# Second and third attention of a decoder: keys in three tiles of 103, two heads to a column group

## The reference

```
# second attention (L0_xattn): 77 keys, q and k normalised per head
q = layernorm((x @ Wq) per head) * sqrt(8);  k, v = (ctx @ Wkv) per head, k layernormed
attn = softmax(q @ k.T);  out = (attn @ v) @ Wp + bp
# third attention (L1_xattn): 77 keys, no bias; masked keys are left out
scores = (x @ W_q.T) @ (ctx @ W_k.T).T / sqrt(8), -inf where mask[key]
attn = softmax(scores), 0 where a row is all masked;  out = (attn @ (ctx @ W_v.T)) @ W_o.T
```

## Time and profile before

| | us |
|---|---|
| median of 3 runs | 399.86 (398.93 to 401.95) |
| the profiled execution, its own time | 399.0 |
| its span, from the first to the last instruction | 397.2 |
| PE busy | 360.5 (91%), 4018 matmul records |
| DVE busy | 275.3 (69%) |
| ACT busy | 220.8 (56%) |
| POOL busy | 144.3 (36%) |
| DMA | 13.86 MB in 16,931 packets, 6,573 of them under 512 B |

### The profile page before, as it was taken

The page is one execution under the profiler, slowest core; times in us unless marked ns, Lnnn a source line. Parts: engine busy times, 40 slices in busy tenths (PEclk is TensorE's granted clock), DMA queues, the critical chain, the costliest instruction groups (busy, mean ns, idle before and its releaser), DMA issues.

```text
span 397.2 us, 10024 instructions
## 1 busy us (share of the span) xinstructions
PE 360.5 (91%) x4018; PEld 243.9 (61%) x4023; DVE 275.3 (69%) x711; ACT 220.8 (56%) x427; POOL 144.3 (36%) x132
## 2 busy tenths in 40 slices
PE   5989998788998989999999999699997999999991
PEld 2556676566775746566767667366774566666670
DVE  6867978655657888789899986755666444544546
ACT  2855568666775355899999951155554522122210
POOL 6939962481442430038789980200112000000002
PEclk9999999999999999999999999999999999999997
DMA  6430000000000000212223210630000000000001
GB/s 176 85 66 2 4 2 2 1 3 3 4 1 2 0 2 2 84 41 96 100 86 113 88 38 2 218 102 3 3 5 0 2 0 0 2 1 0 2 0 54
DMA packets 16931, 13.86 MB, mean 35 GB/s; under 512 B 6573, under 2 KB 14182, under 8 KB 16886
## 3 DMA queue, kind: packets, MB, share of 16 engines
q1 hardware_dynamic: 15586, 12.52, 10.5%
q10 hardware_dynamic: 1299, 0.71, 0.6%
HBM read 12.65 MB, written 0.57 MB: 33 GB/s over the span
## 4 chain that ended last, share of the span: by engine, by line
PE 77%; ACT 9%; DVE 8%; issue 3%; POOL 1%; POOLq 0%; DVEq 0%
PE PS L2000 10%; PE PS L2085 7%; PE PS L2089 7%; PE PS L1560 7%; PE PS L2116 7%; PE PS L1987 5%; PE PS L1499 4%; PE PS L1580 4%; PE PS L1539 4%; ACT att L663 3%; PE PS L1505 3%; PE PS L1629 2%; PE PS L1494 2%; PE PS L1792 2%; PE PS L1563 2%
## 5 line engine op out<-in xcount | busy, mean ns | idle before, releaser
L663 ACT ACTIVATE att<-PS 77x512 f32<-77x512 f32 (+1 forms) x96 | 51.8, 593 | 41.2 <-PE PS L1563 41.2
L1034 DVE TENSOR_REDUCE mxp<-PS 128x4 f32<-128x308 f32 (+1 forms) x96 | 48.2, 537 | 20.3 <-PE PS L1539 20.2
L900 ACT ACTIVATE kM<-PS 128x512 f32<-128x512 f32 x32 | 19.1, 597 | 55.4 <-PE PS L2085 55.4
L507 POOL TENSOR_TENSOR rstd<-ve,neg_half 128x4 f32<-128x4 f32 x6 | 6.2, 1026 | 103.9 <-DVE ve L930 103.9
L513 POOL TENSOR_TENSOR rstd<-ve,neg_half 128x1 f32<-128x1 f32 x24 | 14.3, 594 | 76.8 <-DVE ve L971 76.8
L1438 DVE TENSOR_TENSOR big<-kM,PS 128x512 f32<-128x512 f32 x32 | 21.9, 688 | 27.3 <-PE PS L2089 26.0
L1354 DVE TENSOR_TENSOR_SCAN big<-big,PS 128x768 f32<-128x768 f32 x22 | 38.2, 1747 | 2.5 <-PE PS L1987 2.4
L2085 PE MATMUL PS<-xT,V 128*128 128x512 f32 x64 | 33.0, 597 | 1.1 <-DVE xT L1426 0.8
L2089 PE MATMUL PS<-xT,V 128*128 128x512 f32 x64 | 32.7, 592 | 0.0
L2116 PEld LDWEIGHTS PS<-big 128*128 128x128 f32 x256 | 29.7, 192 | 3.3 <-issue 3.3
L2116 PE MATMUL PS<-big 128*128 128x128 f32 x256 | 29.7, 275 | 0.0
(11 more groups left out here) (362 smaller groups left out, 839.3 us busy)
## 6 DMA issues: line engine op xcount, KB each, us to landing
kM<-Cdram SPq DMA_DIRECT2D x6, 384.0 KB, 3.3
XH<-Cdram SPq DMA_DIRECT2D x5, 384.0 KB, 3.3
xT<-Cdram SPq DMA_DIRECT2D x5, 384.0 KB, 3.5
V<-in_L_ffn_Wg SPq DMA_DIRECT2D x1, 1024.0 KB, 5.2
V<-in_L_ffn_Wu SPq DMA_DIRECT2D x1, 1024.0 KB, 7.8
out_x<-X SPq DMA_DIRECT2D x2, 256.0 KB, 2.5
ctxN<-in_ctx ACTq DMA_DIRECT2D x1, 308.0 KB
X<-in_x ACTq DMA_DIRECT2D x1, 256.0 KB, 4.0
```

Source lines behind the costliest of these rows:

```text
L663: A_(PT[0:nk, i % 2, g], bank4(at.bank("exp", i, g), nk), ACT.Exp, scale=at.scale)\
L1034: V_.tensor_reduce(mxp[:, b % 3, g, 0:J], PS[:, at.bank("max", b, g), 0:J * nk].rearrange("p (j k) -> p j k", j=J), axis=AX.X, op=ALU.max) ...
```

## The change

For `at2` and `at5` the four heads' keys of a group are stored one after the other (308 columns) and cut into three tiles of 103 columns; the third starts at 205, so that it repeats column 205. A tile now holds keys of two heads, or of parts of them. `shifted` does three tiles instead of four, with 103 output partitions instead of 77, and ACT's exponential covers 103 partitions x 384 columns instead of 77 x 512. The value tiles have to follow: each head's values sit at the rows at which its keys lie in the tile (`VALUE_PIECES`), with zeros elsewhere. Context values are now copied to `V0` and from there put into `V2` and `V5` by DMAs of 9-element runs, six for each call of `pack_values`.

In all three attentions two heads share a column group: the value operand of the second starts 9 columns (1 + HD) ahead, so its 9 columns land behind those of the first, and the second product adds to the first. The output has 256 columns instead of 512, `outT` is copied at half the width and transposed in 2 instead of 4, and `weigh` waits for the exponentials in pairs of groups.

The mask of `at5` enters as 12 bf16 products of all 128 rows (mask columns against the identity), one per tile and group. DVE makes `negkey` (128 x 308, in `weights2`), and `maskneg` twice as wide. PE waits for `v2_packed` ahead of the second half of `at2`'s queries, and for `v5_packed` ahead of `at5`.

```
+KT = 103
+KEY_TILES = [0, KT, J * NC - KT]
+TILE_OF = [0, 1, 1, 2]
+VALUE_PIECES = [(0, NC, 0, 0, 0, 0), (0, 26, 1, 77, 0, 1), (26, NC, 1, 0, 1, 1), (0, 52, 2, 51, 2, 0), (52, NC, 2, 1, 3, 0), (0, NC, 3, 26, 3, 1)]
...
+        def pack_values(V, lo, hi, done):
+            for k0, k1, j, r, m, x in VALUE_PIECES:
+                src = V0[k0:k1, lo:hi].rearrange("p b (g j) d -> p (b g) j d", j=J)[:, :, j, :]
+                dst = V[r:r + k1 - k0, lo:hi].rearrange("p b (g m) w -> p (b g) m w", m=J)[:, :, m, (HD + 1) * x:(HD + 1) * (x + 1)]
+                sp.dma_start(dst, src).then_inc(event(done), 16)
+        sp.wait_ge(event("v_ones"), 2)
+        aring.wait_copied(sp, "kv.3")
+        pack_values(V2, 0, B, "v2_packed")
+        sp.wait_ge(event("v_ones"), 6)
+        dring.wait_copied(sp, "v5.0")
+        pack_values(V5, 0, HB, "v5_packed")
         sp.wait_ge(event("proj_copied"), 2)
...
+        aring.wait_copied(sp, "v5.1")
+        pack_values(V5, HB, B, "v5_packed")
...
-                    A_(PT[0:nk, i % 2, g], bank4(at.bank("exp", i, g), nk), ACT.Exp, scale=at.scale)\
+                    A_((PTk if at.packed else PT)[0:at.kt, i % 2, g], bank4(at.bank("exp", i, g), at.kt)[:, 0:nt, :], ACT.Exp,
...
-                    A_(outT[:], bank4(at.out_bank(i - 1)), ACT.Copy).then_inc(at.outT_copied, 1)
+                    A_(outT[:], PS[:, at.out_bank(i - 1), 0:2 * T].rearrange("p (k t) -> p k t", k=2), ACT.Copy)\
...
+            V_.tensor_scalar(negkey[:], selc[:].rearrange("p (j o) -> p j o", o=1).to_broadcast([128, J, NC]), -1.0, None, ALU.mult)
...
                 if at.masked:
+                    for k, lo in enumerate(at.tiles):
+                        keys = maskneg[:].rearrange("p r n -> p (r n)")[:, lo % NC:lo % NC + KT]
+                        for g in range(G):
+                            M_(tile(b, g, k), keys, identb[:], start=(k == 0), stop=False)
+                for k, lo in enumerate(at.tiles):
                     for g in range(G):
...
+                        M_(tile(b, g, k), keys, qT[rows(g), b, :], start=not at.masked, stop=False)
...
-                for g in range(G):
-                    pe.wait_ge(at.exp_ready, G * b + g + 1)
-                    for j in range(J):
-                        ins = M_(PS[32 * j:32 * j + 32, at.out_bank(b), 128 * g:128 * g + 128], at.V[0:nk, b, J * g + j, :],
-                                 PT[0:nk, b % 2, g, j, :], start=True, stop=True)
+                values = at.V.rearrange("p b h w -> p (b h w)")
+                for k in range(2):
+                    pe.wait_ge(at.exp_ready, G * b + 2 * k + 2)
+                    for x in range(2):
+                        for u in range(4):
+                            g, j = 2 * k + u // 2, 2 * (u % 2) + x
+                            lo = (b * H + J * g + j) * VW - (0 if at.packed else x * (HD + 1))
+                            weights = PTk[0:KT, b % 2, g, TILE_OF[j], :] if at.packed else PT[:, b % 2, g, j, :]
+                            ins = M_(PS[32 * u:32 * u + 32, at.out_bank(b), k * T:(k + 1) * T], values[0:at.kt, lo:lo + VW], weights,
+                                     start=(x == 0), stop=(x == 1))
...
-                    for g in range(G):
-                        ins = nc.tensor.transpose(PS[:, at.out_bank(i - 1), 128 * g:128 * g + 128], outT[:, g, :], ident[:])
+                    for k in range(2):
+                        ins = nc.tensor.transpose(PS[:, at.out_bank(i - 1), k * T:(k + 1) * T], outT[:, k, :], ident[:])
...
         def second_queries():
-            pe.wait_ge(event("v_ones"), 2)
+            pe.wait_ge(event("v2_packed"), 16 * len(VALUE_PIECES))
...
-        pe.wait_ge(event("v_ones"), 6)
+        pe.wait_ge(event("v5_packed"), 32 * len(VALUE_PIECES))
```

More of the change, by code:

```diff
@@ L116, in __init__ @@
         self.nk, self.scale, self.kM, self.V = nk, scale, kM, V
+        self.packed = nk == NC
+        self.tiles = KEY_TILES if self.packed else [T * j for j in range(J)]
+        self.kt = KT if self.packed else T
         self.Wo, self.XB, self.Xout, self.masked = Wo, XB, Xout, masked
@@ L490, in _, with value_ones, value_zeros @@
         affine(earlier[:], ALU.is_ge, [[-1, 8], [1, 8]], 0)
[L491 to L498, removed]
+        def value_ones(v):
+            step(P_.memset(v[:, :, :, HD:VW], 0.0))
+            P_.memset(v[:, :, :, HD:HD + 1], 1.0).then_inc(event("v_ones"), 1)
+        def value_zeros(v):
+            P_.memset(v, 0.0).then_inc(event("v_ones"), 1)
         powers = Count(ln_rstd)
@@ L523, in _ @@
         value_ones(V1)
-        value_ones(V2)
+        step(P_.memset(V0[:, :, :, HD:HD + 1], 1.0))
+        value_zeros(V2)
         def residual1():
@@ L577, in value_quarter @@
             if q is not None:
-                value_ones(V5[:, 2 * q:2 * q + 2])
+                value_zeros(V5[:, 2 * q:2 * q + 2])
         attention_pool(at2, value_quarter)
@@ L792, in _ @@
             copy_out(f"srow.{c}", half(Srow, c), bank4, bias=rb2[:])
-        copy_out("v5.1", V5[:, HB:B, :, 0:HD], lambda i: bank4(i, NC).rearrange("p b (h d) -> p b h d", h=H), ACT.Copy)
+        act.wait_ge(event("v2_packed"), 16 * len(VALUE_PIECES))
+        copy_out("v5.1", V0[:, HB:B, :, 0:HD], lambda i: bank4(i, NC).rearrange("p b (h d) -> p b h d", h=H), ACT.Copy)
         table(ACT.Silu)
@@ L1120, in weights5 @@
             loaded(dve, "l5")
-            V_.tensor_scalar(maskneg[:], mask8[:], MASKED, None, ALU.mult)
+            V_.tensor_scalar(maskneg[:], mask8[:].rearrange("p (o k) -> p o k", o=1).to_broadcast([128, 2, NC]), MASKED, None, ALU.mult)
             V_.tensor_scalar(maskrep[:], maskrep8[:], MASKED, None, ALU.mult)
@@ L1255, in _ @@
                 V_.tensor_scalar(X[1][:, b, :], R[:, b, :], mv[:, b, 0:1], rstd[:, b:b + 1], ALU.subtract, ALU.mult)
-        V_.tensor_copy(V5[:, 0:HB, :, 0:HD], bank4(take("v5.0"), NC).rearrange("p b (h d) -> p b h d", h=H)).then_inc(dring.copied, 1)
+        dve.wait_ge(event("v2_packed"), 16 * len(VALUE_PIECES))
+        V_.tensor_copy(V0[:, 0:HB, :, 0:HD], bank4(take("v5.0"), NC).rearrange("p b (h d) -> p b h d", h=H)).then_inc(dring.copied, 1)
         i = take("k5.1")
@@ L1546, in shifted, with tile @@
                 pe.wait_ge(at.flipped_copied, b + 1)
+                def tile(b, g, k):
+                    return PS[0:at.kt, at.bank("exp", b, g), k * T:(k + 1) * T]
                 if at.masked:
-                    for g in range(G):
-                        M_(PS[0:nk, at.bank("exp", b, g), :].rearrange("p (j t) -> p j t", j=J), maskrep[rows(g), 0, :],
-                           first32[rows(g), :].rearrange("p (o t) -> p o t", o=1).to_broadcast([32, J, T]),
-                           start=True, stop=False)
@@ new lines, in shifted @@
+                for k, lo in enumerate(at.tiles):
+                    for g in range(G):
+                        if at.packed:
+                            keys = at.kM[rows(g), :, b, :].rearrange("p j n -> p (j n)")[:, lo:lo + KT]
+                        else:
+                            keys = at.kM[rows(g), k, b, :]
+                        M_(tile(b, g, k), keys, qT[rows(g), b, :], start=not at.masked, stop=False)
+                    for g in range(G):
+                        if at.packed:
+                            pick = negkey[rows(g)].rearrange("p j n -> p (j n)")[:, lo:lo + KT]
+                        else:
+                            pick = negsel[rows(g), k, :]
+                        last = k == len(at.tiles) - 1
+                        ins = M_(tile(b, g, k), pick, upper(flipped)[rows(g), (b - 1) % 2, 0:T], start=False,
+                                 stop=not at.masked or last)
+                        if last:
```

43 lines of the change are left out of this document (17 added, 26 removed).

## The result

| | before | changed |
|---|---|---|
| median, both in one call | 401.94 us (20 runs) | 398.51 us (396.33 to 402.0, 20 runs) |
| profiled execution, its own time | 399.0 | 397.73 |
| its span, mean granted clock | 397.2, 0.993 | 395.9, 0.991 |
| PE busy | 360.5 | 357.2 |

The account below looks back on a forecast made before the run. PE, with its waits between batches, was taken to bound the kernel. At1 -0.15, at2 -3.5, at5 -0.25 and packing at no cost sum to -3.9 us: 399.86 to 395.9 us, range 393.0 to 400.5.

Parts of the forecast that it names:

- mask 0.68 plus 0.09 for the switch: Each at5 batch: 12 whole-array mask products take 0.68 us instead of 0.38, and going to row groups adds 0.09.
- a steady step of at5: One batch of at5: mask +0.30, switch +0.09, three tiles for four -0.22, together +0.17 us.
- DVE as the last to arrive in batches 3 to 5 of at2: In these at2 batches DVE's residual and maximum would end last and take the shorter exponentials' gain away.
- at2's steps 0 to 5: Times from one at2 batch's first tile to the next, batches 0 to 6; forecast 2.07 us less.
- the one on the endings: Last three steps of an attention: chain of exponential, `outT`, transposes gains 1.01 us in at2 and 1.4 in at5.
- step 6: Time from batch 6's first tile to batch 7's; forecast to gain 0.54 us in at2 and 0.23 in at5.
- The flips: PE work near at2's end, named as capping the gain of the third-last step at 0.32 us.
- Step 4 of at2: Time from at2's batch 4 first tile to batch 5's; forecast 0.22 us less, from three tiles for four.
- The packing: Rival: DMAs into V2 and V5 end after PE needs them, up to 409.5 us; chance 0.06 little late, 0.12 clearly late.
- the forecast's even spread: V2's 9,856 packing runs spread evenly over 16 engines, 616 each, taking 9 to 21 us and hidden.
- The mask stream: Rival: at5's mask loads only partly hidden, 0.08 us per product, 2.3 us more in eight batches, 398.2 us; chance 0.17.
- Nothing comes of it: Rival: three tiles run at PE's pace of four and at5 loses what at2 gains, about 398.5 us; chance 0.05.

Follow-up runs that it names:

- e8: Changed kernel with the projection in the flips of step 6 done twice; step 6 grew by 0.22 us in each of at1, at2 and at5.
- e9: Kernel before with the projection in the flips of step 6 done twice; step 6 grew by 0.13 us in at1, 0.12 in at2, 0.09 in at5.
- e7: Changed kernel with DVE taking batch 7's reciprocals ahead of batch 5's residual in at2 and at5; at5 47.62 for 47.77 us, at2 stays at 36.19.
- e2: Changed kernel with at5's mask columns loaded 128 wide instead of 103; at5 47.67 for 47.77 us.
- e3: Changed kernel with `negkey` made behind batch 4 of at1 instead of batch 2; at1's stretch 37.64 us for 37.78.
- e11: The changed kernel run once more, unaltered, beside e10; 0.9917 of the kernel before.
- e4: Changed kernel with the last `weigh` of each attention waiting separately for its last two groups' exponentials; at2 36.19 us as before, at5 47.76 for 47.77.
- e5: Changed kernel with at5 back to four tiles, old mask and unpacked values; 0.9928 of the kernel before, at5 46.79 us.
- e10: Changed kernel with at5 as in e5, `negkey` as in e3, order of e7, `maskneg` dropped; 0.9895 of the kernel before.
- e6: Changed kernel keeping only two heads to a column group: four tiles everywhere, old mask, no packing, no `negkey`; 0.9958 of the kernel before.

## Why the prediction was wrong in size

- **Direction, place and the prices of single operations held.** Tiles 0.31, exponentials, `outT`, mask 0.68 plus 0.09 for the switch (0.78 measured), a steady step of at5 +0.17 (+0.20 measured), DVE as the last to arrive in batches 3 to 5 of at2, at1's steady steps unchanged: all as the trace after shows. at2's steps 0 to 5 were forecast at 2.07 us less and gave 1.98.
- **The step that failed is the one on the endings:** "in the last three steps PE does no scores and the chain is exponential, `outT`, transposes", with 1.0 us beside the tiles in at2, 1.4 in at5 and 0.53 in at1. By the table, step 6 and the end together were forecast at -1.45 in at2 and -1.45 in at5 and came at -1.06 and -0.71. at1, with 0.14 of loss from `negkey` and 0.06 in all, gained 0.08 at its end instead of 0.53. Together 1.6 us are missing; the error of the whole sum is 1.45. I read who ended last, and took the saving from that chain nearly in full. The flips were named as a cap, but only in at2's step 6 and at 0.32 us, a number that no row gave; in at5 I took 0.4 and in at1 0.33 there. The runner-up, the projection, the flips and ACT's copy of them, was 0.09 to 0.13 us behind at step 6 in all three (e8, e9), and no part of the change makes it shorter. That accounts for some 0.7 us of the 1.6. In the very last step the flips left 0.39 of 0.51 in at2 and, with the residual in DVE's order (0.15, e7), 0.22 in at5, by the chains. at1 gained nothing behind step 6, where I had 0.2, and the cause of that was not looked into, nor that of the rest (0.06 us in at2, 0.15 in at5).
- **`negkey`** cost 0.14 and not 0.30, and the wider `maskneg` nothing where I had 0.05 (at1's step 4 is 5.24 in both kernels). Its duration was right (0.31); but PE's scores, which the maximum waits for, were the later ones, and half of it hid.
- **Step 4 of at2** gained 0.08 instead of 0.22: PE waited 0.15 us for the late query (L1637 takes 0.26 us at 93.81 instead of 0.11), for DVE had become the later of the two there as well. That this wait would appear was not in the prediction.
- **The rivals.** The packing wasn't late: its DMAs are issued from 27.55 us on, and the DMA share is 0.78 from 38 to 40 us and nothing of it from 41 on, 32 us ahead of the deadline. But the 13 us don't bear out the forecast's even spread, though they lie between its 9 and 21: from 33 to 35 us only 845 runs were moved, from 30 to 31 alone 1,396, as if some of the six DMAs ran on few engines, which is that rival's premise. What it had wrong is then the price: with its 1,344 runs on the busiest engine, 13 us are 10 ns each (an estimate), not 34. The mask stream wasn't dearer (e2). "Nothing comes of it" had the tiles wrong, though its second half came true in part: at5 loses, but 0.5 us and not all that at2 gains. That its number, about 398.5, is the measured median is luck: it was counted from 399.86, where 2.4 us less would be 397.5. I had at5 at -0.25 with the change and should have asked whether three tiles pay at all there: 0.39 us more of mask and switch against 0.22 less of tiles is a loss in each batch by the prediction's own prices.

## What to carry to other kernels

The saving in a wait is capped by the distance to the wait that comes second. Before a gain at a place is summed, read there when each of the others would have let the engine start, and take the smaller number; a second product put into the runner-up's chain measures the room. And a change that serves two stages is two changes: price it for each, and leave out the stage in which the new cost exceeds the saving.

## What the runs showed of the hardware

- A bf16 weight load of 128 columns and 128 rows takes 98 ns, one of 103 columns 128 ns (e2).
- The granted clock falls to 0.50 for 3 to 7 us in some executions and not in others of the same kernel, and at different places: between 162 and 167 us in the changed kernel's profiled execution, in e3 and in e11, between 140 and 148 us in e2, e4, e5 and e7 to e10, from 254 or 256 to 261 us in e3 and e6, and nowhere on the way in the profiled one of the kernel before. e9 is the kernel before with one product more in each attention, so the change isn't what brings them. In the changed kernel PE had been busy without a gap from 148 us on when the clock fell at 162; the last gaps lie at 140 to 148 us, where PE was busy for 6.4 of 8 us, and the kernel before has such gaps as well (6.7 of 8 us from 142 to 150) and no fall. What sets a fall off stays open. The kernel before takes 399.0 to 399.2 us where the clock's mean is 0.993 or 0.994, 399.9 to 400.5 at 0.990 or 0.991, and 401.8 to 402.3 at 0.980 or 0.982. Most of the spread in both kernels goes with this, and it is as large as the change's effect.
- 9,856 runs of 36 bytes within the on-chip memory, in six DMAs, took 13 us beside everything else.
- Products whose outputs fill four column groups side by side take as long as products that fill two: rounds of 0.11 us either way (e4), so half-filled rounds cost as much as full ones.
